# Layer 1 of a four-layer cross-attention kernel: the split of its weights, made in the first round's steps instead of ahead of them

## The reference

```python
x = L0(x, u)     # self-attention, cross-attention (16 heads of 16), MLP of 1024, layer norms
x = L1(x, u)
x = L2(x, u)     # attention without heads, residual
x = L3(x, u)     # phi, g, theta maps, batch norm

def L1(z1ss, u1ss, Wqkv0, Wqkv1, Winj0, Winj1, Wo, bo, r_w_bias):
    for s, e, Wq, Wi in ((0, 128, Wqkv0, Winj0), (128, 256, Wqkv1, Winj1)):
        h = einsum('od,bdl->bol', Wq, z1ss[:, :, s:e]) + einsum('od,bdl->bol', Wi, u1ss[:, :, s:e])
        chunks.append(h)
    q, k, v = split(concatenate(chunks, axis=2), 3, axis=1)      # 16 heads of 64 features, 256 positions
    score = einsum('bndi,bndj->bnij', q + r_w_bias, k) * 64 ** -0.5
    attn = einsum('bnij,bndj->bndi', softmax(score), v)
    x = einsum('od,bdl->bol', Wo, attn) + bo + z1ss
    return (x - mean(x, 1)) * rsqrt(var(x, 1) + 1e-5)
```

## Time and profile before

| | |
|---|---|
| three runs | 1336.11, 1336.5, 1329.46 us, median 1336.11 |
| the profiled execution | 1332.02 us, span 1330.3 us, mean granted TensorE clock 0.972 |
| busy, share of the span | TensorE 91%, DVE 69%, ACT 62%, POOL 40% |
| layer 0 | to about 468.4 us of the span |
| layer 1 | about 468.7 to 1231 us |
| layers 2 and 3 | the rest |

### The profile page before, as it was taken

The page is one execution under the profiler, slowest core; times in us unless marked ns, Lnnn a source line. Parts: engine busy times, 40 slices in busy tenths (PEclk is TensorE's granted clock), DMA queues, the critical chain, the costliest instruction groups (busy, mean ns, idle before and its releaser), DMA issues. The chain is left out here.

```text
span 1330.3 us, 31116 instructions
## 1 busy us (share of the span) xinstructions
PE 1213.6 (91%) x10914; PEld 996.8 (75%) x10914; DVE 924.4 (69%) x1819; ACT 825.7 (62%) x2479; POOL 532.1 (40%) x519
## 2 busy tenths in 40 slices
PE   4789999999998759999999999999999999997676
PEld 3667788788777558888888888888888888885454
DVE  4788988988977466676766676666667666764333
ACT  4588898888876366565555555655655556553332
POOL 4355664654624013333333333333333333332333
PEclk9899999999999879999999999999999999998799
DMA  3320000000000020000000000000000000000111
GB/s 110 141 103 14 18 14 12 16 12 13 10 5 2 0 79 2 1 10 1 9 1 0 9 0 0 9 0 0 9 0 8 1 0 1 1 1 1 44 50 46
DMA packets 18632, 25.07 MB, mean 19 GB/s; under 512 B 1376, under 2 KB 16992, under 8 KB 18144
## 3 DMA queue, kind: packets, MB, share of 16 engines
q1 hardware_dynamic: 18528, 23.82, 5.5%
HBM read 21.72 MB, written 2.10 MB: 18 GB/s over the span
## 5 line engine op out<-in xcount | busy, mean ns | idle before, releaser
L1199 POOL TENSOR_TENSOR prob<-prob,l_z_inv 128x512 f32<-128x512 f32 x256 | 261.2, 1042 | 457.0 <-DVE l_z_inv L1440 457.0
L1359 ACT ACTIVATE prob<-psum,l_neg_max 128x256 f32<-128x256 f32 x512 | 236.0, 473 | 245.6 <-DVE l_neg_max L1434 231.2
L746 ACT ACTIVATE ring_e<-ring_e,neg_max 128x128 f32<-128x128 f32 x512 | 164.4, 407 | 14.6 <-DVE neg_max L915 14.5
L1434 DVE TENSOR_REDUCE l_neg_max<-psum 128x2 f32<-128x512 f32 x256 | 164.0, 682 | 10.7 <-PE psum L1253 10.7
L1265 PEld LDWEIGHTS psum<-ident,prob 128*128 128x128 f32 x1024 | 109.8, 140 | 49.0 <-issue 45.4
L1281 PE MATMUL psum<-pT,vs 128*64 128x256 f32 x1024 | 138.8, 391 | 6.7 <-DVE aTl L1450 6.6
L1265 PE MATMUL psum<-ident,prob 128*128 128x128 f32 x1024 | 139.9, 280 | 0.0
L1445 DVE COPY pT<-psum 128x512 f32<-128x512 f32 x128 | 88.2, 689 | 50.8 <-PE psum L1265 50.8
L453 POOL TENSOR_TENSOR ring_e<-ring_e,cross_add 128x512 f32<-128x512 f32 x64 | 85.9, 1360 | 91.0 <-DVE ring_e L910 91.0
L453 POOL TENSOR_TENSOR ring_e<-ring_e,self_add 128x512 f32<-128x512 f32 x64 | 86.0, 1358 | 62.2 <-DVE ring_e L910 61.5
L1450 DVE TENSOR_TENSOR aTl<-psum,aTh 128x256 fp32r<-128x256 f32 x128 | 54.4, 425 | 74.2 <-ACT aTh L1374 74.2
(11 more groups left out here) (191 smaller groups left out, 3159.8 us busy)
## 6 DMA issues: line engine op xcount, KB each, us to landing
wz_raw<-wz_in SPq DMA_DIRECT2D x2, 1536.0 KB, 15.1
x_in<-x SPq DMA_DIRECT2D x8, 256.0 KB, 2.8
cT<-ctxT SPq DMA_DIRECT2D x8, 256.0 KB, 2.8
w<-w_in SPq DMA_DIRECT2D x2, 1024.0 KB, 9.1
l_ub<-ctx_in SPq DMA_DIRECT2D x8, 256.0 KB, 2.8
cg<-ctx_in SPq DMA_DIRECT2D x4, 512.0 KB, 4.4
out<-fin SPq DMA_DIRECT2D x4, 512.0 KB, 3.3
wi_raw<-wi_in SPq DMA_DIRECT2D x1, 1536.0 KB, 18.8
```

The lines of the kernel that those rows point to most:

```text
L746: last = nc.scalar.activation(e, e, ACT.Exp, bias=neg_max[:, n % RE, h:h + 1])
L1199: pool.tensor_tensor(e, e, z_inv[:, t % RE, h, :].unsqueeze(2).broadcast_to([P, 2, D]), ALU.mult)\
L1359: last = nc.scalar.activation(prob[:, t % RE, h, qt * D:(qt + 1) * D], score_bank[h][:, qt * D:(qt + 1) * D], ACT.Exp, bias=neg_max[:, t % ...
L1434: nc.vector.tensor_reduce(neg_max[:, t % RE, h, :], score_bank[h].rearrange("p (t c) -> p t c", t=2), AX.X, ALU.max, negate=True).then_inc ...
```

## The change

- The raw `wi` 1 is loaded in layer 0, behind `wi` 0, and the first u at the end of SP's program there, into an `ub` that now exists from the start. For room, `rows` loses its last 256 columns, which layer 0 doesn't read.
- The weights are split in twelve parts (`PARTS`), each of 256 columns of all four tensors: q and k of a head pair together (two blocks of 128 columns), or v of two head pairs. Four parts are made ahead of the steps, the other eight one per step in round 0.
- ACT still makes every hi. DVE makes lo of the two `wz` tensors, POOL lo of the two `wi` tensors. In a step of round 0, ACT's casts stand at the end of the step, DVE's subtractions behind the maxima of the next step, POOL's behind its two multiplications.
- In round 0, each projection waits for the lo of its own part, on two semaphores. The rounds' loop stays.

```diff
@@ -100,10 +100,13 @@
+        ub = sb("l1_ub", [P, 2, D])
+        first_u_in = ctx.enter_context(nc.semaphore("first_u_in"))
...
-        wz0_raw, wz1_raw, wi0_raw = (raw_place.enter_context(nc.sbuf_tensor(n, [P, 3 * NQ], F32)) for n in (
-            "wz0_raw", "wz1_raw", "wi0_raw"))
+        wz0_raw, wz1_raw, wi0_raw, wi1_raw = (raw_place.enter_context(nc.sbuf_tensor(n, [P, 3 * NQ], F32)) for n in (
+            "wz0_raw", "wz1_raw", "wi0_raw", "wi1_raw"))
@@ -161,7 +165,7 @@
             events.append(e)
             return e
 
-        rows = sb("rows", [P, len(ROWS) * D])
+        rows = sb("rows", [P, ROWS["bvpg"]])
         wqkv = sb("wqkv", [P, 2, 3 * D])
         wao = sb("wao", [P, 2, D])
         wq = sb("wq", [P, 2, D])
@@ -385,14 +389,15 @@
             sp.dma_start(cols[:, :], v["cols_in"]).then_inc(w_cols, 16)
             load_weights((wqkv, "wqkv_in", w_qkv))
             sp.dma_start(self_mul[:, :], v["smask"]).then_inc(w_mask, 16)
-            sp.dma_start(rows[:, :], v["rows_in"].partition_broadcast(P)).then_inc(w_rows, 16)
+            sp.dma_start(rows[:, :], v["rows_in"][0:ROWS["bvpg"]].partition_broadcast(P)).then_inc(w_rows, 16)
             next_x(1)
...
             load_weights((wco, "wco_in", w_co), (w1, "w1_in", w_1), (w2, "w2_in", w_2))
-            for w, src, c in ((wz0_raw, "wz_in", 0), (wz1_raw, "wz_in", 1), (wi0_raw, "wi_in", 0)):
+            for w, src, c in ((wz0_raw, "wz_in", 0), (wz1_raw, "wz_in", 1), (wi0_raw, "wi_in", 0),
+                              (wi1_raw, "wi_in", 1)):
                 sp.dma_start(w[:, :], v[src][c * P:(c + 1) * P, :]).then_inc(l1_weights_in, 16)
@@ -400,7 +405,10 @@
                 if g < R0:
                     next_x(g)
             sp.wait_ge(w_mask, 16)
-            sp.wait_ge(l1_weights_in, 48)
+            sp.dma_start(v["ub"][:, :, :], v["ctx_in"].rearrange("b p d -> p b d")[:, 0:2, :])\
+                .then_inc(v["first_u_in"], 16)
+            sp.wait_ge(l1_weights_in, 64)
+            sp.wait_ge(v["first_u_in"], 16)
 
         @block.gpsimd
         def _(pool):
@@ -1079,7 +1087,6 @@
                 pass
             return raw, sb(name, shape, F32R)
 
-        wi1_raw, wil1 = place("wil1", [P, 3 * NQ])
         wo_raw, wol = place("wol", [P, PAIRS, P])
         wz = [[sb(f"wzh{c}", [P, 3 * NQ], F32R) for c in range(2)], [wzl0, wzl1]]
         wi = [[sb(f"wih{c}", [P, 3 * NQ], F32R) for c in range(2)], [wil0, wil1]]
@@ -1105,14 +1113,28 @@
         pv_bank = psum[:, 4, 0:D]
         wo_bank = psum[:, 7, :]
 
-        HALF = 3 * NQ // 2
-        parts = [tuple(w[:, h * HALF:(h + 1) * HALF] for w in (hi, lo, raw)) for h in range(2)
-                 for hi, lo, raw in ((wz[0][0], wz[1][0], wz0_raw), (wz[0][1], wz[1][1], wz1_raw),
-                                     (wi[0][0], wi[1][0], wi0_raw), (wi[0][1], wi[1][1], wi1_raw))]
+
+
+        PARTS = ["qk0", "v0", "qk1", "qk2", "v1", "qk3", "qk4", "v2", "qk5", "qk6", "v3", "qk7"]
+        AT_ONCE = 4
+        tensors = ((wz[0][0], wz[1][0], wz0_raw), (wz[0][1], wz[1][1], wz1_raw),
+                   (wi[0][0], wi[1][0], wi0_raw), (wi[0][1], wi[1][1], wi1_raw))
+
+        def part(w, n):
+            if PARTS[n][0] == "v":
+                return w[:, 2 * NQ + int(PARTS[n][1]) * D:2 * NQ + (int(PARTS[n][1]) + 1) * D]
+            at = int(PARTS[n][2]) * P
+            return w[:, 0:2 * NQ].rearrange("p (t c) -> p t c", t=2)[:, :, at:at + P]
+
+        def rounded(name):
+
+            n = "v" + name[1] if name[0] == "v" else "qk" + name[1]
+            return 2 * (PARTS.index(n) + 1)
+
         wo_hi, wo_lo, wo_in_place = (w[:, :, :].rearrange("p h o -> p (h o)") for w in (*wo, wo_raw))
-        wi_in, wo_in = sem("l1_wi_in"), sem("l1_wo_in")
-        hi_made, lo_made, wo_hi_made, wo_lo_made = (sem(n) for n in (
-            "weights_hi_made", "weights_lo_made", "wo_hi_made", "wo_lo_made"))
+        wo_in = sem("l1_wo_in")
+        hi_made, z_lo_made, i_lo_made, wo_hi_made, wo_lo_made = (sem(n) for n in (
+            "weights_hi_made", "z_weights_lo_made", "i_weights_lo_made", "wo_hi_made", "wo_lo_made"))
 
 
 
@@ -1181,11 +1203,6 @@
                 sp.dma_start(ub[:, :, :], v["ctx_in"].rearrange("b p d -> p b d")[:, bass.ds(i * NB, NB), :])\
                     .then_inc(u_in.sem, 16)
 
-            load_u(0)
-            for h in range(2):
-                sp.dma_start(wi1_raw[:, h * HALF:(h + 1) * HALF],
-                             v["wi_in"][P:2 * P, h * HALF:(h + 1) * HALF]).then_inc(wi_in, 16)
-                sp.wait_ge(wi_in, 16 * (h + 1))
             sp.dma_start(wo_raw[:, :, :], v["wo_in"].rearrange("(h r) o -> r h o", r=P)).then_inc(wo_in, 16)
             with sp.Fori(1, R1) as i:
                 sp.wait_ge(*zu_lo.at(i - 1, 1))
@@ -1203,16 +1220,26 @@
                 pool.wait_ge(*work.out(name, i))
                 pool.tensor_tensor(rstd[:, :], var_eps[:, :], half_neg[:, 0:4], ALU.pow).then_inc(rstd_done.sem, 1)
 
+            def rest_part(n):
+                for m, (hi, lo, raw) in enumerate(tensors[2:4]):
+                    pool.wait_ge(hi_made, len(tensors) * n + m + 3)
+                    pool.tensor_tensor(part(lo, n), part(raw, n), part(hi, n).bitcast(F32), ALU.subtract)\
+                        .then_inc(i_lo_made, 1)
+
             def body(i, first, last):
                 for t in range(STEPS):
                     for h in range(2):
                         norm(i, t, h)
+                    if first and t < len(PARTS) - AT_ONCE:
+                        rest_part(t + AT_ONCE)
                     if t == T_READ:
                         inverse_std(i, "var")
 
             def tail(i):
                 inverse_std(i, "k0")
 
+            for n in range(AT_ONCE):
+                rest_part(n)
             pool.wait_ge(wo_hi_made, 1)
             pool.tensor_tensor(wo_lo, wo_in_place, wo_hi.bitcast(F32), ALU.subtract).then_inc(wo_lo_made, 1)
             rounds(pool, body, tail)
@@ -1223,6 +1250,9 @@
 
             def project(i, name):
                 ps = work.psum(name)
+                if isinstance(i, int) and i == 0:
+                    pe.wait_ge(z_lo_made, rounded(name))
+                    pe.wait_ge(i_lo_made, rounded(name))
                 pe.wait_ge(*work.free(name, i))
                 pe.wait_ge(*zu_lo.at(i, 1))
                 for c in range(2):
@@ -1346,7 +1376,6 @@
                 spread(i, "q1", 1)
 
             for name in AHEAD:
-                pe.wait_ge(lo_made, len(parts) // 2 if name in ("q0", "k0") else len(parts))
                 project(0, name)
             rounds(pe, body, tail)
 
@@ -1389,9 +1418,16 @@
                     "p b (c l) -> p c b l", c=2)).then_inc(zu_hi.sem, 1)
 
             def round_u(i):
-                act.wait_ge(*u_in.at(i))
+                if isinstance(i, int) and i == 0:
+                    act.wait_ge(first_u_in, 16)
+                else:
+                    act.wait_ge(*u_in.at(i - 1))
                 nc.scalar.copy(zu[0][:, 1, :, :, :], ub[:, :, :].rearrange("p b (c l) -> p c b l", c=2))\
                     .then_inc(zu_hi.sem, 1)
+
+            def round_part(n):
+                for hi, lo, raw in tensors:
+                    nc.scalar.copy(part(hi, n), part(raw, n)).then_inc(hi_made, 1)
 
             def body(i, first, last):
                 for t in range(STEPS):
@@ -1407,6 +1443,8 @@
                     for name, r in fills(i, t, last):
                         if name in split:
                             round_work(r, name)
+                    if first and t + AT_ONCE < len(PARTS):
+                        round_part(t + AT_ONCE)
 
             def tail(i):
                 copy_turned(i - 1, STEPS - 1)
@@ -1414,13 +1452,10 @@
                 round_heads(i - 1, STEPS - 1)
 
             round_z(0)
-            act.wait_ge(l1_weights_in, 48)
-            for n, (hi, lo, raw) in enumerate(parts):
-                if n % 4 == 3:
-                    act.wait_ge(wi_in, 16 * (n // 4 + 1))
-                nc.scalar.copy(hi, raw).then_inc(hi_made, 1)
-                if n == 3:
-                    round_u(0)
+            round_part(0)
+            round_u(0)
+            for n in range(1, AT_ONCE):
+                round_part(n)
             for name in AHEAD[:2]:
                 round_work(0, name)
             act.wait_ge(wo_in, 16)
@@ -1510,10 +1545,18 @@
                 to = y[:, b, :] if first else xs[:, bass.ds((i - 1) * NB + b, 1), :].rearrange("p a d -> p (a d)")
                 nc.vector.tensor_tensor(to, y[:, b, :], ps, ALU.mult).then_inc(work.reads(name), 1)
 
+            def rest_part(n):
+                for m, (hi, lo, raw) in enumerate(tensors[0:2]):
+                    dve.wait_ge(hi_made, len(tensors) * n + m + 1)
+                    nc.vector.tensor_tensor(part(lo, n), part(raw, n), part(hi, n).bitcast(F32), ALU.subtract)\
+                        .then_inc(z_lo_made, 1)
+
             def body(i, first, last):
                 for t in range(STEPS):
```

(25 more changed lines are left out.)

## The result

| | before | after |
|---|---|---|
| median of 13 runs each | 1334.76 us (1329.46 to 1336.5) | 1338.5 us (1334.25 to 1340.9) |
| profiled execution | 1332.02 us, span 1330.3 | 1336.88 us, span 1335.2, mean granted clock 0.969 |

The ratio is 1.003 with a 95% interval of 1.0019 to 1.0042: no faster, and measurably a little slower. The forecast was 1324.5 us with a range of 1316 to 1333; the result lies above it.

What follows compares the result with a forecast made beforehand. TensorE's idle and slow-clock time where layer 0 ends and layer 1 begins was taken as the bound. -7.0 - 3.65 + 0.9 = -9.75 us gave 1324.5 us, midway between two starting points' results; range 1316 to 1333.

Steps and rivals of the forecast that it cites:

- Start, -7.0 us: Start of layer 1: rounding a first small part lets TensorE's first projection start at 472.3 instead of 479.29, -7.0 us.
- First projections, -3.65 us: First projection to scores of step 1: no second gap or clock fall, 10.65 us instead of 14.30, -3.65 us.
- First round, +0.9 us: Layer 1, steps 0 to 7: eight parts made there cost 0.1 us each, plus 0.1 for fuller waits.
- The spare times: Steps of the first round: ACT's casts and TensorE's transposes each fit with about 0.2 us to spare.
- Layer 0, 0 us: Layer 0: the extra wi1 load, smaller rows, first u and wo's rounding were claimed to cost 0 us.
- the fuller waits of 21 projections: First round of layer 1: the added waits at 21 projections were allowed 0.1 us in all.
- its two starting points: Whole kernel before: profiled execution 1332.02 us and median of three runs 1336.11, giving 1322.3 and 1326.4; the middle was taken.
- the clock did fall: Rival at q0 and k0: clock stays full, 3.0 us instead of 5.2, total -11.95, 1322.3 us; chance 0.07.
- the steps gave back 0.1 us: Rival in the first round: eight steps each lose 0.3 to 0.8 us beyond the allowance, 1327 to 1331 us; chance 0.15.
- the start moved: Rival at layer 1's start: something unchanged sets it, TensorE's start stays, time 1334 to 1337 us; chance 0.04.
- The slower one: Rival in steps 1 to 8: DVE's and POOL's subtractions serialise before the reciprocals, +4.7 us, 1339 us; chance 0.04.
- The remark that the split over two engines gains nothing: Subtractions on DVE and POOL: an exclusive lock prevents gain side by side; without the split rest_u ends 0.4 us sooner.

Runs made afterwards that it cites:

- 10: The changed kernel with all four subtractions of a part on VectorE, counted on one semaphore, zu_lo waited for once; 1322.93 us, 0.9926 of the kernel before.
- experiments 7: The changed kernel with zu_lo waited for only at q0 in round 0, and all four subtractions of a part on VectorE; 1320.12 us, 0.99 of the kernel before.
- experiment 5: The kernel before with 24 empty TensorE instructions right behind the loop over rounds 1 to 6; 1332.82 us, 0.9997 of the kernel before.

## Why the prediction was wrong, point by point

- *Start, -7.0 us.* Right: idle 4.67 us against the forecast 4.4. It was released by GpSimd's second subtraction, not by zul: I had taken 0.6 us for each of the two, going by the columns, and beside VectorE they take 0.98 and 1.17. With all subtractions on VectorE (10) the idle time is 4.26 us, released by zul; those 0.4 us are what the prediction said the split costs.
- *First projections, -3.65 us.* Right within 0.4: 481.94 - 470.90 = 11.04 us against 14.30, which is -3.26. The clock stayed halved in q0 and nearly all of k0 (0.50 from 468.6 to 475.4) and didn't fall a second time.
- *First round, +0.9 us.* Between the scores of step 1 and the first mark lie 162.78 us after and 162.66 before: +0.1. The spare times read from the earlier trace rows held, though VectorE stood still beside GpSimd for 0.2 us a subtraction.
- *Layer 0, 0 us.* Nothing in these runs points to a cost: its wait rows are those of before.
- **The step that failed** is the last half sentence of the first round: "0.1 for the fuller waits of 21 projections". I priced the waits where they stand. That was right there, and it left out that they are instructions in front of a loop. They moved the loop, and at each of five jumps back TensorE's branch lasted 4.0 to 4.5 us instead of 0.21 while instructions were loaded; each pass took 1.7 to 3.8 us longer, three of them by a slow clock too: +13.9 us, more than all that was won. No sentence of the prediction gives a price to loading instructions.
- The sum without that term, 1324.5 us, is what the kernels without the displacement show: 1324.31, 1324.39 and 1322.93. The three terms measure -6.8, -3.3 and +0.1, in sum -9.9 us against -9.75. So what the forecast says of the start and of the first round was right, and a term was missing. (The middle of its two starting points is 1334.1, not 1334.2, and the forecast from it 1324.3; nothing hangs on that.)
- *The rivals.* None happened: the clock did fall, the steps gave back 0.1 us, and the start moved. The slower one (two engines' subtractions in series, 1339 us) comes close to the measured 1338.5 by accident: the first round, its place, lost 0.1 us of its 15.4. The remark that the split over two engines gains nothing was right, also for the exclusive lock of the Trainium skill (SBUF — State Buffer, "Who interferes with whom"): the 621 ns against 416 agree with it, and experiments 7 and 10 lose nothing without the split.
- The last 220 us (behind the last mark) take 217.65 us before, 220.15 after, and 224.0 in experiment 5, which has the code of before there. That part varies by several us with the granted clock in layer 2, and I read nothing from it.

What is shown: the position of the loop decides whether queue 8 loads in every pass, and the jump into a loading pass is where TensorE stands. What is argued only: that the limit is seven blocks of 256. The counts fit it if the unseen part ahead is about 55 instructions (with 8 empty ones the body then ends just at a block's end: 21 + 8 + 55 + 1708 = 7 x 256), but no run varied the body's length. Nor does it say why a loading pass takes nine packets, when a body across eight blocks needs eight.

## What to carry to other kernels

Compare the instruction queues' packets of two kernels before anything else is explained, and look at TensorE at each jump back of a loop: idle time there, booked on whatever semaphore came last, together with packets in every pass, is the loop being loaded again. Packets alone prove nothing: queue 14 had five a pass before, at no cost that can be seen, with passes of 91.28 us. Count the instructions that a change adds in front of a long loop, waits above all, since each wait on a further semaphore can be an instruction of its own; put several producers on one semaphore, or wait once where one wait covers all. And when the expected gain is seen at its own place but not in the total, set marks that come once per pass and subtract: the loss was found in code that the change doesn't touch.

## What the runs showed of the hardware

- TensorE's loop of 1708 instructions stays loaded or is loaded again in a pass (nine packets of 16 KB, and a branch of 4.0 to 5.0 us instead of 0.21, of which 2.2 to 3.4 us are idle time of the matmuls), according to a shift of some ten instructions.
- A loading pass is 1.7 to 2.1 us longer, and 3.2 to 4.2 us longer where the granted clock falls to 0.50 behind the idle time, which it did in nine of the seventeen.
- An empty instruction that counts a semaphore takes TensorE's sequencer 0.15 us (29.3 us for 200 that stand together). 24 in front of the loop delay its first jump by 2.45 us; 24 where TensorE waits anyway cost nothing measurable.
- A subtraction of 256 columns takes VectorE 416 ns with no subtraction of GpSimd beside it and 621 ns with one, and GpSimd's takes 826 in the mean; with 1536 columns GpSimd takes 3.9 to 5.0 us, and VectorE 1.75 ahead of GpSimd's and 5.0 beside them.
